# A two-layer decoder on one core: expert tiles loaded in pairs into ten slots of dead buffers, four output slots, and the recurrence's pace chosen by the planner

## What is computed

```python
x = x + L0_attn(layernorm(x))       # rms norm, gated linear recurrence (scan), 256 wide
x = x + L0_xattn(layernorm(x), ctx) # 16 heads, softmax over 64 context positions
x = x + L0_ffn(layernorm(x))        # x W + x V_r C
x = x + L1_attn(layernorm(x))       # an LSTM of 20 cells over 512 steps gives the centre and
                                    # width of Gaussian weights over positions; context = w x
x = x + L1_xattn(layernorm(x), ctx) # as above, with a gate on the weights
x = x + L1_ffn(layernorm(x))        # 8 experts, the best one of each token:
...
indices = jnp.argmax(weights, axis=-1)
h = jnp.einsum('bsd,ehd->bseh', x, w_fc)
h = jnp.where(h >= 0, h, 0.5 * h)
h = h * h
out = jnp.einsum('bseh,edh,bse->bsd', h, w_proj, onehot)
```

## Time and profile before

| | us |
|---|---|
| median of 3 runs | 3188.12 |
| lowest and highest | 3178.17, 3192.34 |
| the profiled execution | 3191.33 |
| its span, first to last instruction | 3189.5 |
| stage 1 (347 to 729 us of the span) | 382 |
| stage 2 (729 to 1369) | 640 |
| stage 3 (1369 to 1997) | 628 |
| stage 4 (1997 to 2467) | 470 |
| stage 5, three bodies with tiles (2467 to 2958) | 491 |
| stage 5, last body (2958 to 3050) | 92 |
| stage 6 (3050 to the end) | 139 |

### The profile page before, as it was taken

The page is one execution under the profiler, slowest core; times in us unless marked ns, Lnnn a source line. Parts: engine busy times, 40 slices in busy tenths (PEclk is TensorE's granted clock), DMA queues, the critical chain, the costliest instruction groups (busy, mean ns, idle before and its releaser), DMA issues.

```text
span 3189.5 us, 39732 instructions
## 1 busy us (share of the span) xinstructions
PE 2584.9 (81%) x11385; PEld 1542.6 (48%) x11385; DVE 1893.2 (59%) x6517; ACT 853.2 (27%) x2341; POOL 1317.4 (41%) x1372
## 2 busy tenths in 40 slices
PE   5799896977778778778778787999998868887945
PEld 3466453543636354635354545544544535544533
DVE  4576787768685767586768686645655414242311
ACT  0233242332232233223232332212222212122211
POOL 0363342324443345334444453423432545555534
PEclk9999896978786887678878786999899889899965
DMA  4110101020101110201010101111111253433032
GB/s 160 54 62 13 49 12 38 1 71 14 48 24 39 33 53 25 58 20 58 20 57 20 57 14 47 34 41 34 33 40 36 71 119 90 127 96 100 27 92 81
DMA packets 195337, 164.88 MB, mean 52 GB/s; under 512 B 52913, under 2 KB 188171, under 8 KB 194896
## 3 DMA queue, kind: packets, MB, share of 16 engines
q1 hardware_dynamic: 182352, 137.55, 14.6%
q0 software_dynamic: 12800, 25.27, 2.8%
HBM read 118.81 MB, written 51.80 MB: 53 GB/s over the span
## 4 chain that ended last, share of the span: by engine, by line
PE 36%; issue 21%; DVE 19%; POOL 12%; DMA 6%; SPq 3%; ACT 2%; POOLq 0%; DVEq 0%; ACTq 0%
PE p L775 4%; PE p L869 4%; PE p L832 4%; PE p L808 4%; PE p L769 3%; DVE l_xnat L1185 3%; PE p L786 3%; DMA out<-xy,xid 3%; DMA xw<-in_w_proj 3%; PE p L822 2%; POOL l_scratch L1547 2%; PE pg L841 2%; DVE ln_stats L1160 2%; PE p L849 2%; POOL l_scratch L1542 2%
## 5 line engine op out<-in xcount | busy, mean ns | idle before, releaser
L1521 POOL TENSOR_TENSOR ln_rstd<-ln_ve,neghalf 128x4 f32<-128x4 f32 x96 | 98.2, 1023 | 714.6 <-DVE ln_ve L1169 713.2
L1535 POOL TENSOR_TENSOR l_kbd<-l_kg,headmask 128x512 f32<-128x512 f32 x256 | 266.8, 1052 | 305.5 <-PE p L808 210.7
L1465 DVE SCALAR_TENSOR_TENSOR uin<-gates 16x20 f32<-16x20 f32 x512 | 175.5, 343 | 283.4 <-ACT gates L987 281.5
L832 PEld LDWEIGHTS p<-l_vg,l_scratch 128*128 128x128 f32 x2048 | 282.2, 215 | 75.0 <-issue 36.6
L987 ACT ACTIVATE gates<-pg 16x80 f32<-16x80 f32 x512 | 114.9, 224 | 761.0 <-PE pg L841 759.4
L1542 POOL TENSOR_TENSOR l_scratch<-l_scratch,l_mx 128x512 f32<-128x512 f32 x256 | 265.3, 1042 | 117.5 <-DVE l_mx L1215 116.7
L832 PE MATMUL p<-l_vg,l_scratch 128*128 128x34 f32 x2048 | 292.7, 296 | 15.9 <-ACT l_scratch L1016 6.8
L769 PE MATMUL p<-ident,l_xnat 128*128 128x128 f32 x1024 | 202.0, 339 | 123.2 <-DVE l_xnat L1185 122.0
L841 PE MATMUL pg<-wcat,slots 128*16 128x80 f32 x1024 | 177.2, 260 | 150.9 <-DVE slots L1477 149.0
L808 PE MATMUL p<-l_kbd,l_qT 128*128 128x512 f32 x512 | 275.6, 628 | 10.9 <-DVE l_scratch L1211 9.7
L841 PEld LDWEIGHTS pg<-wcat,slots 128*16 128x16 f32 x1024 | 59.0, 97 | 387.9 <-DVE slots L1477 238.5
(11 more groups left out here) (209 smaller groups left out, 4723.6 us busy)
## 6 DMA issues: line engine op xcount, KB each, us to landing
xln<-xln_dram SPq DMA_DIRECT2D x40, 512.0 KB, 4.4
l_vg<-v_dram SPq DMA_DIRECT2D x32, 544.0 KB, 4.0
x_dram<-l_xres SPq DMA_DIRECT2D x32, 512.0 KB, 3.6
xw<-in_w_fc SPq DMA_DIRECT2D x84, 128.0 KB, 2.2
xw<-in_w_proj SPq DMA_DIRECT2D x84, 128.0 KB, 2.5
l_kg<-k_dram SPq DMA_DIRECT2D x32, 256.0 KB, 4.3
xln_dram<-l_xnat SPq DMA_DIRECT2D x16, 512.0 KB, 3.0
l_xres<-x_dram SPq DMA_DIRECT2D x16, 512.0 KB, 5.5
```

The costliest lines, as they stand in the source:

```text
L832: i = pe.matmul(o_bank[l][:, q * VW:(q + 1) * VW], w.exT[:, j, p, :], w.vg[:, b, q * VW:(q + 1) * VW], start=True, stop=True)
L1465: dve.scalar_tensor_tensor(uin[:, :], gates[:, 0:20], 1.0, gates[:, 60:80], ALU.add, ALU.mult)
L1535: pool.tensor_tensor(w.kbd[b % 2][:, j, :, :], w.kg[:, j, b:b + 1, :].broadcast_to([P, NE, SK]), headmask[:, :].rearrange("p (a o) -> p a ...
```

## The change

- Tiles: ten slots instead of four, four output slots instead of two. The slots get no memory of their own: the weights go into matrices that only layer 0 used (`wA` to `wF`, `wQ0`, `wO0`) and the rows into lane 0's activation buffers, all of which nobody reads after stage 3. The memsets of the old row slots go.
- SP loads tiles in pairs (six DMAs in a row), and the semaphores of loads and rows count pairs: both gathers wait for all six loads, and the turn of either tile for both gathers.
- The planner is given new durations for the tile's steps (5.6 us for a pair of loads on SP, 2.6 us of POOL per tile), 7.0 us instead of 3.0 for what a DMA delivers, and 2.8 us instead of 3.5 per tile in stage 5.
- The spread of the recurrence is no longer a number per stage. The planner tries 72 to 144 us in steps of 8 and keeps the plan that it finds shortest. It takes 112 us for the first three bodies of stage 2 and 120 for its last, 120 and 104 in stage 3, and 72 for all of stage 4. Stage 0, stage 1 and the last body of stage 5 keep their order word for word.
- Stage 6 joins the stages with fillers.
- Three semaphores of the scan become one (`s_small`), so the scan waits once less.

```diff
-TILE_SLOTS = 4
+TILE_SLOTS, OUT_SLOTS = 10, 4
...
+        steps += [
+            ("clock", "due", p, 2 * every, [("due", p - 1)]),
+            ("sp", "mload", p, 5.6, [("due", p - 1), ("mexpert", 2 * p + 1 - TILE_SLOTS), ("mscatter", 2 * p + 1 - TILE_SLOTS)]),
+            ("dma", "mids", p, 0.1, [("mload", p)])]
+        steps += [("pool", "mgather", k, 1.3, [("mids", p), ("madd", k - TILE_SLOTS)]) for k in (2 * p, 2 * p + 1)]
+        steps += [("dma", "mrows", p, 0.1, [("mgather", 2 * p + 1)])]
     for k in range(count):
         steps += [
-            ("clock", "due", k, every, [("due", k - 1)]),
-            ("sp", "mload", k, 1.5, [("due", k - 1), ("mexpert", k - TILE_SLOTS), ("mscatter", k - TILE_SLOTS)]),
-            ("dma", "mids", k, 0.1, [("mload", k)]),
-            ("pool", "mgather", k, 1.3, [("mids", k), ("madd", k - TILE_SLOTS)]),
-            ("dma", "mrows", k, 0.1, [("mgather", k)]),
-            ("pe", "mturn", k, 0.25, [("mrows", k), ("mland", k - 1)]),
-            ("act", "mland", k, 0.4, [("mturn", k), ("mhidden", k - 2)]),
+            ("pe", "mturn", k, 0.45, [("mrows", k // 2), ("mland", k - 1)]),
+            ("act", "mland", k, 0.38, [("mturn", k), ("mhidden", k - 2)]),
             ("pe", "mhidden", k, 0.5, [("mland", k), ("mleaky", k - 1)]),
-            ("act", "mrelu", k, 0.3, [("mhidden", k), ("msquare", k - 1)]),
-            ("dve", "mleaky", k, 0.25, [("mrelu", k)]),
+            ("act", "mrelu", k, 0.28, [("mhidden", k), ("msquare", k - 1)]),
+            ("dve", "mleaky", k, 0.3, [("mrelu", k)]),
             ("act", "msquare", k, 0.3, [("mleaky", k), ("mexpert", k - 2)]),
             ("pe", "mexpert", k, 0.5, [("msquare", k), ("madd", k - 1)]),
-            ("dve", "madd", k, 0.42, [("mexpert", k), ("mscatter", k - 2)]),
+            ("dve", "madd", k, 0.42, [("mexpert", k), ("mscatter", k - OUT_SLOTS)]),
             ("pool", "mscatter", k, 1.3, [("madd", k)])]
...
-HOPS = {"pe": 0.22, "act": 0.2, "dve": 0.18, "pool": 0.1, "sp": 0.2, "dma": 3.0, "clock": 0.0}
-
-PACE = {0: (0.0, 4.0, 0.4), 1: (96.0, 16.0, 0.6), 2: (128.0, 4.0, 0.3), 3: (140.0, 0.0, 0.4), 4: (112.0, -18.0, 0.35),
-        5: (0.0, 22.0, 0.4), 6: (0.0, 0.0, 0.4)}
+HOPS = {"pe": 0.22, "act": 0.2, "dve": 0.18, "pool": 0.1, "sp": 0.2, "dma": 7.0, "clock": 0.0}
+
+PACE = {0: (4.0, 0.4), 1: (16.0, 0.6), 2: (4.0, 0.3), 3: (0.0, 0.4), 4: (-18.0, 0.35), 5: (22.0, 0.4), 6: (0.0, 0.4)}
...
-TILE_EVERY = 3.5
-
-
-IDLE, FILL, WARM = 0.3, 0.9, (0, 4, 5)
+TILE_EVERY = 2.8
+
+
+IDLE, FILL, WARM = 0.3, 0.9, (0, 4, 5, 6)
 
 
 def planned(stage, ahead):
 
-    recurrence, (spread, lead, window) = P // bodies(stage), PACE[stage]
+    spreads = range(72, 152, 8) if 1 <= stage <= NC_ else (0,)
+    return min((planned_at(stage, ahead, spread) for spread in spreads), key=lambda plan: plan[0])[1]
+
+
+def planned_at(stage, ahead, spread):
+
+    recurrence, (lead, window) = P // bodies(stage), PACE[stage]
...
-    return kept
+    return max(end.values()), kept
...
-        xw = [sb(f"xw{i}", [P, 2 * D]) for i in range(TILE_SLOTS)]
-        xg = [sb(f"xg{i}", [P, 2 * D]) for i in range(TILE_SLOTS)]
+        whole = lambda w: w[:, :, :].rearrange("p h n -> p (h n)")
+        xw = [whole(w) for w in (wA, wB, wC, wD, wOut, wF, wQ[0], wO[0])]
+        parts = lambda w: [w[:, i:i + 2 * D] for i in range(0, 4 * D, 2 * D)]
+        done = tiles[0]
+        xw += parts(whole(done.xres))
+        xg = parts(whole(done.xnat)) + parts(whole(done.xT)) + parts(whole(done.qT))
+        xg += [t for w in done.kbd for t in parts(w[:, :, :, :].rearrange("p h a k -> p (h a k)"))]
         xid = [sb(f"xid{i}", [P, 2], I32) for i in range(TILE_SLOTS)]
         xgT = [sb(f"xgT{i}", [P, D]) for i in range(2)]
         xh = [sb(f"xh{i}", [P, P]) for i in range(2)]
         xq = [sb(f"xq{i}", [P, P]) for i in range(2)]
-        xy = [sb(f"xy{i}", [P, D]) for i in range(2)]
+        xy = [sb(f"xy{i}", [P, D]) for i in range(OUT_SLOTS)]
 
         ctxA = xln[:, :, :, :].rearrange("p i b d -> p (i b d)").rearrange("p (h b k) -> p h b k", h=NH, b=B)
         kv_w = [(tiles[l].xres[:, 0:NH, :], tiles[l].xres[:, NH:2 * NH, :]) for l in range(2)]
...
-            def load_expert(q):
-
-                s = q % TILE_SLOTS
-                if q >= TILE_SLOTS:
-                    sp.wait_ge(m_expert, q - TILE_SLOTS + 1)
-                    sp.wait_ge(o_store[q % 2], 16 * ((q - TILE_SLOTS) // 2 + 1))
-                early = EARLY * TILES[0]
-                j = q if q < early else q - early
-                which = sp.value_load(tile_i[0:1, 0, j:j + 1], min_val=0, max_val=NE - 1)
-                start = sp.value_load(tile_i[0:1, 1, j:j + 1], min_val=0, max_val=ID_ROWS - P)
-                sp.dma_start(xid[s][:, :], id_dram[bass.ds(start, P), :]).then_inc(m_in[s], 16)
-                sp.dma_start(xw[s][:, 0:D].rearrange("p (h n) -> p h n", h=NH), halves(a["w_fc"])[:, :, bass.ds(which * P, P)]
-                             ).then_inc(m_in[s], 16)
-                sp.dma_start(xw[s][:, D:2 * D], a["w_proj"][:, bass.ds(which, 1), :].rearrange("p o n -> p (o n)")).then_inc(m_in[s], 16)
+            def load_experts(first):
+
+                for q in (first, first + 1):
+                    s = q % TILE_SLOTS
+                    if q >= TILE_SLOTS:
+                        sp.wait_ge(m_expert, q - TILE_SLOTS + 1)
+                        sp.wait_ge(o_store[(q - TILE_SLOTS) % OUT_SLOTS], 16 * ((q - TILE_SLOTS) // OUT_SLOTS + 1))
+                    early = EARLY * TILES[0]
+                    j = q if q < early else q - early
+                    which = sp.value_load(tile_i[0:1, 0, j:j + 1], min_val=0, max_val=NE - 1)
+                    start = sp.value_load(tile_i[0:1, 1, j:j + 1], min_val=0, max_val=ID_ROWS - P)
+                    sp.dma_start(xid[s][:, :], id_dram[bass.ds(start, P), :]).then_inc(m_in[s // 2], 16)
+                    sp.dma_start(xw[s][:, 0:D].rearrange("p (h n) -> p h n", h=NH), halves(a["w_fc"])[:, :, bass.ds(which * P, P)]
+                                 ).then_inc(m_in[s // 2], 16)
+                    sp.dma_start(xw[s][:, D:2 * D], a["w_proj"][:, bass.ds(which, 1), :].rearrange("p o n -> p (o n)")).then_inc(m_in[s // 2], 16)
...
-                            load_expert(TILES[0] * (r if stage == NC_ + 1 else EARLY) + index)
+                            load_experts(TILES[0] * (r if stage == NC_ + 1 else EARLY) + 2 * index)
...
-                    pe.wait_ge(m_rows[s], 16 * turns + 16)
+                    pe.wait_ge(m_rows[s // 2], 32 * turns + 32)
...
-            for t in xg:
-                dve.memset(t[:, :], 0.0)
...
-                    dve.wait_ge(l0.a_ready, 2 * n + 2)
+                    dve.wait_ge(l0.s_small, 4 * n + 3)
                     dve.wait_ge(l0.u_ready, 2 * n + 2)
-                    dve.wait_ge(l0.s_carry, n + 1)
...
-                if positive(q - 1):
-                    dve.wait_ge(m_give, q - 1)
-                    dve.wait_ge(o_store[k % 2], 16 * halved)
-                dve.tensor_tensor(xy[k % 2][:, :], banks[0][2][:, 0:D], xg[k % TILE_SLOTS][:, 0:D], ALU.add).then_inc(m_added, 1)
+                if positive(q - OUT_SLOTS + 1):
+                    dve.wait_ge(m_give, q - OUT_SLOTS + 1)
+                    dve.wait_ge(o_store[k % OUT_SLOTS], 16 * written)
+                dve.tensor_tensor(xy[k % OUT_SLOTS][:, :], banks[0][2][:, 0:D], xg[k % TILE_SLOTS][:, 0:D], ALU.add).then_inc(m_added, 1)
...
-                    pool.wait_ge(m_in[s], 48 * turns + 48)
+                    pool.wait_ge(m_in[s // 2], 96 * turns + 96)
```

35 lines of the change are left out of this document (18 added, 17 removed).

## The result

The changed kernel takes 3052.5 us (median of 4 runs, 3032.9 to 3055.9); the kernel before took 3190.2 beside it. The ratio is 0.956, with a 95% interval of 0.951 to 0.961. The forecast was 2956, its range 2890 to 3045: the sign was right and the size was not. The profiled execution took 3050.8 us, 91 more than the 2959 forecast in its terms.

What follows compares the result with a forecast made beforehand. No one engine bounds all stages: coupled PE and DVE in 2 and 3, fillers in 4, tile waits in 5. Terms -41 - 92 - 66 - 22 - 11 = -232 give 2959 profiled, 2956 median; range 2890 to 3045.

Steps and rivals of the forecast that it cites:

- Stage 3 (-22, got +8): Stage 3: eighteen LSTM steps leave the tails and cost less among other work; -22 us, bounds -45 and +10.
- stage 2 (-11, got +6): Stage 2: nine LSTM steps leave the tails; -11 us, bounds -30 and +15.
- the price of an LSTM step among other work: Stages 2 and 3: a moved step costs DVE 0.87 us where it has no gap, against 1.87 in the tail.
- Stage 4 (-66, got -38): Stage 4: 327 fillers of 0.216 us go, 71 us, of which 5 are left; -66 us, bounds -45 and -80.
- The bounding step: Stage 4: fillers covering planned idle time have become the body's length, 56.3 us of a 116 us body.
- Stage 5 (-92, got -89): Stage 5, three tile bodies: PE's tile waits and 153 fillers go; -92 us, bounds -50 and -110.
- its last body (0, got 0): Stage 5, last body without tiles: keeps its order, so no change, 0 us.
- Rival 3: Stage 5: tiles 10 to 19 wait for scatters, so that stage saves only about 50 us; 2998 us, chance 17%.
- Stage 6 (-41, got -32): Stage 6: ten slots and fillers leave SP's load issue as next limit; -41 us, bounds -50 and +10.
- the distance of 2.82 us a tile: Stage 6: SP issues each tile's loads 2.82 us after the last, putting its last load at 3124.
- rival 4: Stages 2 and 3: moved steps meet a DVE with no gap, +10 and +15 instead of -33; about 3014, chance 8%.
- Rivals 1 and 2: Thinner clock in stages 4 and 5, 3089, 7%; clock collapse over stages 4 to 6, slower than before, 3211, 3%.

Runs made afterwards that it cites:

- the third kernel: Changed kernel with the old paces in stages 2 and 3, plus ACT writing one LSTM gate into the cell's bank instead of SBUF: 2908.2 us, ratio 0.910.

## Why the prediction was off, step by step

**Stage 3 (-22, got +8) and stage 2 (-11, got +6).** The step that failed is the price of an LSTM step among other work: "Among other work each costs DVE its own 0.87 wherever DVE has no gap", 0.64 us in all. The trace has what it really cost. In the first three bodies of stage 3 four steps left the tail, 10.2 us became 2.9, and the other work ended 11.4, 10.5 and 11.2 us later, 2.8 us for each moved step. Among that are the holds, 36 us that became 55: the earlier trace rows is a step of the tail, where POOL stands still, and its 0.17 us for the first instruction is 0.356 in the mean of stage 3 as the kernel before already had it. With the holds gone stage 3 gains 20 us (16 against the kernel that differs in the pace alone) where the term had 22, so its other part, the 0.87 us where DVE has no gap, is not contradicted. For stage 2 the term fails even then: 0 instead of -11 (-6 against the third kernel). PE's busy time there rose from 481 to 500 us for the same instructions as its clock fell from 0.81 to 0.79; why the new order of stage 2 has the lower clock stays open. Both results of stage 2 are inside the bounds that I gave (-30 to +15), and the +8 of stage 3 is inside its own.

**Stage 4 (-66, got -38).** This is outside its bounds, -45 to -80. The fillers taken out did go: PE's busy time fell by 59 us, 71 for 327 fillers less some 12 that its own work grew by at a clock of 0.90 instead of 0.95. But PE's idle time rose by 21 (36 to 57), where I had left 5. Of a body of 109 us PE is busy 96, and each body begins with 4 us of PE idle and 13.7 us at half clock. The bounding step, that fillers are the length of a body, held for 38 of the 66 us; then DVE, held 30 us instead of 22, was late. With the holds gone the term is right within 1 us, and the clock is 0.95.

**Stage 5 (-92, got -89), its last body (0, got 0).** The mechanism came as forecast: SP runs ahead and PE's waits for tiles shrink. Rival 3 (ten slots don't fill) is out. PE's waits at the turn are 7.8 us, under the 15 that the prediction named. But the number is right partly by luck. The terms were 62 us less of waits (3 us of new ones) and 33 us less of fillers. In the busy times PE's idle time in the tile bodies fell by 42 us only (98 to 56), since some 35 us of new waits stand at the products behind the turn, and its busy time fell by 45 (393 to 348), 12 more than the fillers, while the clock rose from 0.89 to 0.94. The two errors cancel.

**Stage 6 (-41, got -32).** The fillers kept the clock at 0.95, as forecast. The term that was mis-sized is the distance of 2.82 us a tile. It was taken from the first three distances of the stage, which are as short in the changed kernel; over the whole stage it became 3.14: 23 x 0.32 = 7 of the missing 9 us.

**The rivals.** Of the four the one that came nearest is rival 4 (stages 2 and 3 don't gain, 8%, 3014), and it was still 38 us short: stage 4 lost 28 us to moved steps as well, for which I had a forecast of its own. Its cause was also another one, a DVE with no gap; what the runs show is a DVE held behind POOL. Rivals 1 and 2 (the clock) did not come: 0.90 and 0.94 are above the 0.80 and 0.75 at which they decide. Still the clock costs the kernel much in a stage where I had not looked for it: fillers alone take 46 to 56 us off stage 2.

**The range.** I added the bounds of the stages "as independent". They weren't: stages 2, 3 and 4 rest on one price for a step among other work, and when that was wrong all three moved up together, by 17, 30 and 28 us, stage 4 past its bound of 21. Added in line, the three are 26 + 32 + 21 = 79 us, which is 3035 before the bounds of stages 5 and 6 are put on top: such a range would have held 3052.
